# Quantisation batches of four sequences, six sequences normalised by ScalarE alone, six residuals on GpSimd, and a new order of all queues

## The reference, cut to what matters

```python
xn = (x - mean(x)) / sqrt(var(x) + 1e-5)          # over the 128 features

# branch 1: recurrence
r, k, v = split(xn @ W_rkv + b_rkv, 3)
r, k = sigmoid(r), exp(k)
kv = k * v
gamma, lam = exp(nu_log + gamma_log) - 1, exp(-exp(nu_log))
u1, u2 = scan(lam, kv), scan(lam, k)              # y[t] = lam * y[t-1] + u[t]
s = ((u1 + gamma*kv) / (u2 + gamma*k + 1e-6) * r) @ W_o + b_o

# branch 2: quantised product, scales over blocks of 32 features
xd = dequantise(quantise_fp6(xn)); wd = dequantise(quantise_fp6(W))
g = silu(xd @ wd.T + bias)

out = x + s * g
```

## Time and profile before

| | |
|---|---|
| median of three runs | 118.81 us (118.44 to 119.31) |
| profiled execution | 118.47 us, its span 116.7 us, 1669 instructions |
| PE busy | 107.5 us, 92% of the span |
| DVE busy | 105.6 us, 91% |
| ACT busy | 101.7 us, 87% |
| POOL busy | 100.8 us, 86% |
| PE's granted clock | 0.992 of full on average |
| HBM read, written | 4.53 MB, 4.19 MB |

### The profile page before, as it was taken

How to read it: one execution, slowest core, us unless ns; L and a number is a source line. 1 busy time by engine, 2 the same in 40 slices (tenths; PEclk the granted TensorE clock), 3 DMA queues, 4 the chain that set the end, 5 groups by cost and what they waited for, 6 DMA issues and landing times.

```text
span 116.7 us, 1669 instructions
## 1 busy us (share of the span) xinstructions
PE 107.5 (92%) x403; PEld 59.1 (51%) x403; DVE 105.6 (91%) x171; ACT 101.7 (87%) x176; POOL 100.8 (86%) x110
## 2 busy tenths in 40 slices
PE   4947999979999999999999999999999999999970
PEld 4934435535455546445473544755545554545550
DVE  0539999999999999999998999999999899999891
ACT  4049899999999999999999999999998999899700
POOL 2189978999999999798999999999999999997800
PEclk9999999999999999999999999999999999999996
DMA  2869960000002000200022100021111021020047
GB/s 70 244 199 404 386 248 0 0 6 3 6 0 90 0 0 0 90 0 0 18 77 90 65 25 0 0 89 43 53 41 54 0 90 72 18 90 0 0 184 265
DMA packets 6024, 8.81 MB, mean 76 GB/s; under 512 B 1536, under 2 KB 1920, under 8 KB 6016
## 3 DMA queue, kind: packets, MB, share of 16 engines
q1 hardware_dynamic: 5040, 8.72, 20.7%
q10 hardware_dynamic: 976, 0.00, 0.5%
HBM read 4.53 MB, written 4.19 MB: 75 GB/s over the span
## 4 chain that ended last, share of the span: by engine, by line
PE 74%; ACT 12%; DVE 3%; DMA 3%; POOL 3%; issue 1%; DVEq 1%; ACTq 0%; POOLq 0%
PE taken_ps L1020 32%; PE turned_ps L1001 11%; PE so_ps L1076 10%; PE v_ps L1048 10%; PE num_ps L1062 5%; PE so_ps L1082 5%; ACT xn L764 5%; DMA x_all<-in_L_attn_inputs_dram 3%; ACT L747 2%; POOL rstd L316 2%; ACT k L792 2%; ACT recept L799 2%; DVE x_all L553 2%; PE turned_ps L1076 1%; DVE gate L548 1%
## 5 line engine op out<-in xcount | busy, mean ns | idle before, releaser
L1020 PE MATMUL taken_ps<-xnT,wrkv_sb 128*128 128x512 f32 x64 | 31.8, 597 | 0.3 <-ACT k L792 0.3
L764 ACT ACTIVATE xn<-x_all,shift,rstd 128x128 f32<-128x128 f32 x48 | 20.1, 497 | 5.7 <-POOL shift L336 5.7
L384 POOL TENSOR_TENSOR mixed<-mixed,den 128x1024 f32<-128x1024 f32 (+1 forms) x10 | 19.3, 1934 | 2.0 <-ACT den L817 1.2
L527 DVE TENSOR_TENSOR_SCAN num_ps<-own_ps,kv 128x512 f32<-128x512 f32 x16 | 19.4, 1215 | 0.0
L378 POOL TENSOR_TENSOR den<-den,gk 128x1024 f32<-128x1024 f32 (+1 forms) x10 | 19.2, 1930 | 0.1
L517 DVE TENSOR_TENSOR_SCAN den<-own_ps,k 128x512 f32<-128x512 f32 x16 | 19.1, 1207 | 0.0
L747 ACT ACT_TABLE_LOAD x14 | 18.0, 1283 | 0.9 <-PEq L1243 0.7
L481 DVE BATCH_NORM_STATS2 stats<-x_all 128x6 f32<-128x256 f32 x32 | 11.7, 417 | 6.2 <-DMA x_all<-in_L_attn_inputs_dram 6.2
L1048 PE MATMUL v_ps<-xnT,wrkv_sb 128*128 128x512 f32 x32 | 16.4, 595 | 0.0
L1020 PE MATMUL taken_ps<-xdT,wdT 128*128 128x512 f32 x32 | 16.2, 599 | 0.1
L355 POOL TENSOR_TENSOR q<-xn,inv_scale 128x1024 fp8e4<-128x1024 f32 (+1 forms) x10 | 15.7, 1571 | 0.4 <-DVE inv_scale L500 0.4
(11 more groups left out here) (73 smaller groups left out, 188.2 us busy)
## 6 DMA issues: line engine op xcount, KB each, us to landing
x_all<-in_L_attn_inputs_dram SPq DMA_DIRECT2D x16, 256.0 KB, 6.6
out_dram<-x_all SPq DMA_DIRECT2D x16, 256.0 KB, 2.0
wrkv_sb<-in_L_attn_W_rkv_dram SPq DMA_DIRECT2D x1, 192.0 KB, 4.4
wf_sb<-in_L_ffn_weight_dram SPq DMA_DIRECT2D x1, 64.0 KB, 6.3
wo_sb<-in_L_attn_W_o_dram SPq DMA_DIRECT2D x1, 64.0 KB, 6.1
cols<-in_L_attn_nu_log_dram ACTq DMA_DIRECT2D x1, 0.5 KB, 3.8
cols<-in_L_attn_gamma_log_dram ACTq DMA_DIRECT2D x1, 0.5 KB, 4.0
cols<-in_L_attn_b_o_dram ACTq DMA_DIRECT2D x1, 0.5 KB, 4.6
```

The costliest lines, as they stand in the source:

```text
L384: nc.gpsimd.tensor_tensor(ring(mixed, n, m), ring(mixed, n, m), ring(den, n, m), ALU.mult)\
L527: nc.vector.tensor_tensor_scan(num_ps[:, :], lam_ps.to_broadcast([P, W]), kv[:, n % KS, :], 0.0, ALU.mult, ALU.add).then_inc(num_scanned, 1)
L764: ins = nc.scalar.activation(xn[:, n % XN, j * D:(j + 1) * D], x_all[:, n, j * D:(j + 1) * D], ACT.Identity, bias=shift[:, t:t + 1], scale ...
L1020: nc.tensor.matmul(taken_ps[i % 2][:, :], weights, moving, start=True, stop=True).then_inc(filled, 1)
```

## The change

All engines' lists are written anew. What differs besides order:

- `QUANT_BATCHES`: six batches instead of nine, three of them of four sequences. `XN` is 8 instead of 4.
- `STAT_BATCHES`: the last two batches of four sequences are one of eight, so one `rough_std`, `deviations` and `inv_std` go away.
- `ACT_ALONE`: ACT normalises all four tiles of sequences 3, 5, 7, 9, 11, 13; POOL does none of them.
- `RES_POOL`: six sequences instead of four, so ten residuals instead of twelve are DVE's.
- gamma kv on DVE for 2, 5, 7, 9, 11, 13 only; PE does the other ten.
- `wf` is loaded third and `wrkv` sixth; `ffn_weights` on DVE and `transpose_wd` on PE are at the head of their lists.
- ACT's list has twelve table loads instead of fourteen.
- Ring orders `TURNS` and `TAKEN` follow the new lists; `STORES` swaps 10 and 11.

```diff
-    XN, Q, XD, XNT, XDT, KS, DEN, MIX, REC, GAT = 4, 4, 4, 8, 8, 6, 6, 6, 8, 8
+    XN, Q, XD, XNT, XDT, KS, DEN, MIX, REC, GAT = 8, 4, 4, 8, 8, 6, 6, 6, 8, 8
-    STAT_BATCHES = [(0, 1), (1, 2), (2, 4), (4, 8), (8, 12), (12, 16)]
-    QUANT_BATCHES = [(0, 1), (1, 2), (2, 4), (4, 6), (6, 8), (8, 10), (10, 12), (12, 14), (14, 16)]
+    STAT_BATCHES = [(0, 1), (1, 2), (2, 4), (4, 8), (8, 16)]
+    QUANT_BATCHES = [(0, 1), (1, 2), (2, 4), (4, 8), (8, 12), (12, 16)]
-    RES_POOL = [2, 5, 8, 11]
+    RES_POOL = [1, 3, 5, 6, 8, 10]
-                if POOL_TILES:
-                    engine.wait_ge(xn_pool, n + 1 - FIRST)
+                if n not in ACT_ALONE:
+                    engine.wait_ge(xn_pool, n + 1 - FIRST - sum(m <= n for m in ACT_ALONE))
+        ACT_ALONE = [3, 5, 7, 9, 11, 13]
-            sp.dma_start(wrkv_sb[:, :], w_rkv).then_inc(wrkv_loaded, 16)
+            sp.dma_start(wf_sb[:, :], w_ffn).then_inc(wf_loaded, 16)
             load(2)
             load(3)
-            sp.dma_start(wf_sb[:, :], w_ffn).then_inc(wf_loaded, 16)
+            sp.dma_start(wrkv_sb[:, :], w_rkv).then_inc(wrkv_loaded, 16)
...
-                for j in ACT_TILES:
+                for j in range(TPP) if n in ACT_ALONE else ACT_TILES:
...
```

More of the change, by code:

```diff
@@ L426, in _ @@
-            denominator(2, 2)
-            normalise(9)
             quantise(6, 2)
-            normalise(10)
+            ratio(2, 2)
+            dequantise(6, 2)
+            residual(1)
+            normalise(14)
             denominator(4, 2)
[L431 to L437, removed]
+            normalise(15)
+            denominator(6, 2)
+            ratio(4, 2)
@@ L630, in _ @@
+            scan_num(2)
+            statistics(15)
+            gamma_kv(2)
+            key_values(5)
+            receive(2)
+            block_maxima(3)
+            scan_num(3)
+            key_values(6)
             block_scales(3)
             inverse_scales(3)
[L632 to L636, removed]
+            receive(3)
             gating(0)
-            key_values(4)
-            scan_den(3)
+            scan_num(4)
@@ L640, in _ @@
+            scan_den(4)
             residual(0)
-            statistics(12)
-            key_values(5)
-            receive(2)
+            scan_den(5)
+            scan_den(6)
+            receive(4)
+            gating(1)
+            scan_num(5)
+            gamma_kv(5)
+            key_values(7)
+            receive(5)
+            scan_den(7)
+            gating(2)
+            scan_num(6)
+            residual(2)
             block_maxima(4)
-            statistics(13)
-            statistics(14)
@@ L647, in _ @@
-            scan_num(3)
+            receive(6)
+            gating(3)
+            key_values(8)
+            scan_den(8)
             block_scales(4)
             inverse_scales(4)
[L650 to L659, removed]
+            scan_num(7)
+            gating(4)
+            key_values(9)
@@ L660, in _ @@
+            gamma_kv(7)
+            residual(4)
+            receive(7)
+            scan_num(8)
+            gating(5)
+            scan_den(9)
+            scan_den(10)
+            key_values(10)
+            scan_den(11)
+            gating(6)
+            receive(8)
+            scan_num(9)
+            key_values(11)
+            gamma_kv(9)
+            receive(9)
+            scan_num(10)
+            gating(7)
             block_maxima(5)
-            receive(4)
+            residual(7)
@@ L662, in _ @@
+            receive(10)
+            key_values(12)
             block_scales(5)
             inverse_scales(5)
[L664 to L699, removed]
@@ L700, in _ @@
-            block_scales(7)
-            inverse_scales(7)
-            gating(7)
+            scan_num(11)
+            gamma_kv(11)
+            gating(8)
             scan_den(12)
             scan_den(13)
[L705 to L713, removed]
-            scan_den(14)
-            receive(11)
@@ L716, in _ @@
-            gating(9)
-            scan_num(12)
-            key_values(13)
-            scan_den(15)
[L720 to L727, removed]
+            receive(11)
+            scan_num(12)
+            gating(9)
+            key_values(13)
+            scan_den(14)
+            residual(9)
+            receive(12)
+            key_values(14)
@@ L728, in _ @@
+            scan_num(13)
+            key_values(15)
+            gamma_kv(13)
+            gating(10)
+            receive(13)
+            scan_den(15)
             scan_num(14)
-            key_values(15)
             gating(11)
             receive(14)
+            residual(11)
             scan_num(15)
-            gamma_kv(15)
             receive(15)
@@ L1132, in _ @@
             ffn(3)
-            values(6)
+            project(1)
+            transpose_xd(4)
+            receptance(6)
+            receptance(7)
+            untranspose(1)
             transpose_xn(9)
-            keys(6)
-            keys(7)
-            untranspose(1)
-            transpose_xd(4)
+            transpose_xn(10)
+            ffn(4)
+            project(2)
+            transpose_xd(5)
             keys(8)
-            values(7)
-            keys(9)
-            gamma_kv(4)
-            transpose_xd(5)
+            untranspose(2)
@@ L1160, in _ @@
+            untranspose(3)
+            values(9)
+            keys(11)
             project(4)
+            transpose_xd(7)
+            ffn(5)
+            untranspose(4)
+            values(10)
             ffn(6)
+            project(5)
             transpose_xn(12)
[L1163 to L1166 removed]
+            receptance(8)
+            untranspose(5)
             transpose_xd(8)
[L1168 to L1170 removed]
@@ L1171, in _ @@
-            ffn(8)
-            values(11)
-            gamma_kv(8)
-            transpose_xn(13)
-            transpose_xd(9)
-            untranspose(5)
-            receptance(9)
-            receptance(10)
-            project(6)
-            ffn(9)
+            receptance(9)
+            gamma_kv(8)
+            project(6)
+            ffn(7)
+            receptance(10)
+            values(11)
+            untranspose(6)
+            receptance(11)
+            transpose_xn(13)
+            ffn(8)
@@ L1194, in _ @@
             project(8)
-            ffn(10)
-            receptance(13)
-            untranspose(8)
-            receptance(14)
-            values(13)
-            project(9)
-            transpose_xd(12)
-            keys(15)
-            receptance(15)
-            untranspose(9)
-            gamma_kv(12)
-            values(14)
+            receptance(13)
+            transpose_xn(15)
+            untranspose(8)
+            values(13)
+            ffn(9)
+            transpose_xd(11)
+            project(9)
@@ L1207, in _ @@
+            keys(15)
+            gamma_kv(12)
+            untranspose(9)
+            values(14)
+            receptance(14)
+            ffn(10)
+            project(10)
+            values(15)
+            receptance(15)
+            transpose_xd(12)
+            transpose_xd(13)
             ffn(11)
-            transpose_xd(13)
-            project(10)
+            untranspose(10)
+            ffn(12)
             transpose_xd(14)
-            ffn(12)
-            untranspose(10)
+            project(11)
```

360 lines of the change are left out of this document (176 added, 184 removed), and 16 rows, old and new, of tables (TAKEN, TURNS).

## The result

| | before | after |
|---|---|---|
| median of the runs | 118.66 us (118.44 to 119.31) | 119.97 us (119.66 to 120.25) |
| ratio after to before | | 1.011, 95% interval 1.007 to 1.014 |
| span of the profiled execution | 116.7 us | 118.5 us |
| `project(15)` starts | 110.37 us | 112.12 us |

The change costs 1.3 us, about 1.1%. The forecast was 120.2 us. The profiled execution of the changed kernel took 120.25 us, 0.28 more than its median.

What follows compares the result with a forecast made beforehand. PE was taken as the bound, all else close behind. PE's sum of +1.45 us and a hand walk's +1.1 gave +1.4, hence 119.9 us profiled and 120.2 us median; range for 8 in 10: 118.0 to 122.4.

Steps and rivals of the forecast that it cites:

- The signs: What would show it right: 20 gamma kv products, chain on PE from 25 us, DVE 4 to 5 us less, twelve table loads.
- The counts: Work per engine over the whole kernel: PE +1.72 less 0.27 hidden, DVE 4.6 us less, ACT +0.5, POOL -1.6.
- PE is the bound: From 25.06 to 110.07 us the chain never leaves PE; its work before `project(15)` is 95.8 us, gaps 5.1.
- ACT +0.5, beside PE: ACT's tiles, copies out, table loads and rough deviation sum to +0.5 us, off the path that sets the end.
- Covered: At the start, first key values at 15.8 instead of 13.29 us cost nothing; PE needs them only at about 16.9.
- forecast sum of +1.45: On PE up to `project(15)`: two more gamma kv products +1.72, `wd` turn hidden in the idle start -0.27 us.
- The head: Before PE's first turn: `transpose_wd` hidden in idle time, -0.27 us; `wrkv` loaded sixth costs 0, with 1.5 us of cover.
- POOL as the bound: Slower rival: POOL's ratios delay `project(15)`, batches of four add 1.0 us; +2.6 us, 121.4 us, chance 0.18.
- DVE as the bound: Faster rival: DVE's queue makes PE late everywhere; its relief closes 3.3 of 5.1 us of gaps; -1.8, 117.0 us, chance 0.15.

## Why the prediction was right, and where its reasons were not

- **The number.** 120.2 forecast, 119.97 measured; the span 118.1 and 118.5; `project(15)` +1.1 to +1.45 and +1.75. By the prediction's own count that is +1.45 of PE's work and 0.5 of gaps (5.6 instead of 5.1 us), less 0.18 by which the first turn came earlier.
- **The signs.** Of those named for "right", the 20 product instructions and the 12 table loads came. The chain on PE from 25 us on did not, nor did DVE's 4 to 5 us less.
- **The counts.** All but one held: PE's +1.72, ACT's +0.5 (0.7 found), POOL's -1.6 (1.6). DVE's busy time fell by 1.9 instead of 4.6. The instructions went as said, but the durations summed over DVE fell by 3.2 only: three pairs of scale and reciprocal less gave 0.9 and not 1.5, as the pairs of larger batches take longer, and the one instruction that forms `gam_diag` took 0.86 instead of 0.29. The rest, from 3.2 to 1.9, is overlap: an instruction overlaps the next, so that one removed takes less out of the busy time than it lasts.
- **"PE is the bound"**, read from a chain that stays on PE from 25 to 110 us. This step failed. Taking 2.1 us from PE in the kernel before gives 0.1 us; adding 1.72 costs 0.84; taking 1.72 away again in the changed kernel, at DVE's expense, gives nothing. PE is one of three engines that are full in the middle of the kernel, and the chain, which at each step names one releaser, showed PE since PE had no gap. A chain on one engine showed that more work on it would cost something. It did not show that less would gain.
- **"ACT +0.5, beside PE".** This step failed as well. ACT's additions to the kernel before are paid nearly one to one (+2.2 or +1.8 us for 2.3). The 0.7 us that ACT has more in the changed kernel would by that price be 0.55 to 0.7 us of the loss, as an estimate. Taking work off ACT in the changed kernel is worth far less, 0.5 us for 2.2, so the price does not hold both ways.
- **"Covered"**, of the late first key values. That cover is not there: what they are late by, from 15.5 to 16.2 us in profiles of the same start, is found again in full at 43 us, since DVE's own queue has no gap in which to make it up (18.97 of 19 us busy from 25 to 44).
- **The sum.** By the single runs on the kernel before: two products with DVE relieved +0.84, ACT +0.55 to 0.7 (estimate), head -0.42. That is 1.0 to 1.1 of the 1.5 us. The remaining 0.4 to 0.5 us would be the new order and the batches of four; they were not tried alone, and single prices need not add up in a kernel with four full engines. So what makes the change slower is accounted for in part and not shown as a whole. That the forecast sum of +1.45 came so near is in good part luck: it charged PE in full, where half was due, and ACT with nothing.
- **The head.** Expected to gain by hiding 0.27 us of PE's work, it brings 0.42 alone, and mostly by something else. `wf` landed 3.9 us after its issue, `wd` was turned at 7.1 us, ahead of PE's first turn, and nothing waited for `wrkv`. But 0.26 of the gain stand at the first turn already: in all ten profiles with the new head DVE's first statistics start at 4.08 to 4.18 us, in the four with the old one at 4.35 to 4.59. Why the first sequence lands earlier, though its load goes ahead of either weight, no run tells.
- **POOL as the bound.** As the one engine that sets the end it is excluded: 2.2 us less on POOL changes nothing. As the one that holds the stretch before 69 us it is not: there that dose gained 0.43, which is lost behind it. The rule of the Trainium skill named there ("GPSIMD Engine Reference", Engine selection) holds as to the duration, 1.28 us against 0.68, but does not bear on the end here.
- **DVE as the bound**, the faster rival: DVE's relief did not pay. 2.2 us less again give 0.2. It decides where its answers are placed, though: two gamma kv ahead of two gatings cost as much as they took off PE.

## What to carry to other kernels

When several engines are about 90% busy, an unbroken chain on one of them tells that adding to it costs something, at most the addition, and not what relieving it gains. Take a dose of work off each engine in turn, giving it to none, before deciding whose load to shift, and hold the starts of a few instructions against each other to see where the gain stands and where it is lost. Price a shift by the engine that receives it (here ACT, nearly one to one) as well as by the one relieved. Of the parts tried alone the new head was the only one that paid, and it could be had without the rest.

## What the runs showed of the hardware

In some executions of the same kernel PE's granted clock falls in the first 15 us. Of the 65 timed executions of the kernel before beside the experiments, 48 had a mean clock of 0.99 or more and took 118.3 to 118.95 us, 17 had 0.986 or less and took 119.4 to 119.8. The profile of the lighter PE on the kernel before was of the second kind. Two of its windows (the clock stands behind POOL's busy time), and then one step of its chain of waits:

```profile
9.50:15.00 5.50, 5.14 (x14) 2.63 (x14) 4.27 (x16) 4.20 (x12) 5.18 (x9) 0.69 1.06 396
15.00:20.00 5.00, 4.79 (x18) 2.35 (x17) 4.72 (x13) 4.94 (x11) 2.58 (x9) 1.00 0.27 99
```

```profile
11.40 1.79 PE taken_ps L1020 x2
```

The first keys product takes 1.79 us there and 1.09 in the chain of the kernel before's own profile: the clock is at the lower of its two levels, 1.2 instead of 2.4 GHz, for part of the stretch. Ahead of it PE had been through its warm-up and then idle for 1.65 us; the kernel before's own profile, at full clock, was idle there for 2.27. The 1.1 us are lost once and never made up. Of 52 timed executions of the changed kernel and its variants, whose turn of `wd` lies in that idle stretch, one was of this kind; of 21 of the kernel before with that head, three; of the 90 of the kernel before and its variants with the old head, 26. Whether the turn of `wd` is the cause was not tried by itself.
